# Mask and decay scores as one product of 88 rows a half, key-value products of 32 output rows

## What is computed

```python
log_f = log_sigmoid(fg); cs = cumsum(log_f)           # per head, over the tokens
log_D = where(tril, cs_s - cs_t, -inf) + ig_t         # mask and decay scores
D_mat = exp(log_D - max(log_D))
C = (q k^T / sqrt(32)) * D_mat
h = C / (max(|sum C|, exp(-max)) + 1e-6) @ v          # 8 heads of 32
x = x + tanh(g) * layernorm(h) * ln_scale
```

## Time and profile before

| | |
|---|---|
| three runs | 786.97, 788.75, 788.55 us; median 788.55 |
| profiled execution | 790.31 us, its span 788.5 us |
| PE busy | 678.9 us, 86% (weight loads 545.5, 69%) |
| DVE busy | 527.2 us, 67% |
| POOL busy | 404.8 us, 51% |
| ACT busy | 386.1 us, 49% |
| constants and gates | 0 to 57 us |
| hand-over | 57 to 85 us |
| attention loop, slots 0 to 31 | 85 to 295 us |
| routing | 295 to 350 us |
| experts | 350 to 788 us |

### The profile page before, as it was taken

One profiled execution on the slowest core, in us unless ns is written; L12 is line 12 of the kernel. 1 busy time (PEld: TensorE's weight loads), 2 busy tenths in 40 slices (PEclk: granted clock), 3 DMA queues, 4 the chain that ended last, 5 costly groups with the idle time before them and its releaser, 6 DMA issues.

```text
span 788.5 us, 17816 instructions
## 1 busy us (share of the span) xinstructions
PE 678.9 (86%) x6018; PEld 545.5 (69%) x6018; DVE 527.2 (67%) x1389; ACT 386.1 (49%) x973; POOL 404.8 (51%) x402
## 2 busy tenths in 40 slices
PE   1983889998899874068999999999999999999993
PEld 1541556665566663047998989988989899889893
DVE  8716899899998877964555565555555555655551
ACT  3533677777777763154344444343444443434441
POOL 5024499897989991021244453453444535444423
PEclk9995655557655655569999999999999999999997
DMA  9813789986998861173597897897988977969752
GB/s 283 270 37 122 198 267 263 297 280 208 298 300 254 269 209 54 29 307 108 166 289 238 265 281 253 232 315 213 281 259 245 291 253 234 315 200 305 231 147 49
DMA packets 85817, 179.70 MB, mean 228 GB/s; under 512 B 14881, under 2 KB 48546, under 8 KB 85730
## 3 DMA queue, kind: packets, MB, share of 16 engines
q1 hardware_dynamic: 63202, 140.10, 56.2%
q0 software_dynamic: 13824, 18.43, 10.8%
q10 hardware_dynamic: 8704, 20.06, 6.5%
HBM read 140.93 MB, written 38.67 MB: 228 GB/s over the span
## 4 chain that ended last, share of the span: by engine, by line
PE 57%; POOL 20%; issue 9%; DVE 9%; ACT 2%; DMA 2%; SPq 1%; POOLq 0%; DVEq 0%; ACTq 0%
PE bank L1096 49%; POOL whl L483 8%; POOL x L717 3%; POOL x L720 3%; POOL vp L561 3%; POOL qE L577 2%; PE bank L304 2%; PE bank L1090 2%; PE bank L307 2%; POOL kw L569 2%; DVE R L991 1%; PE bank L317 1%; DMA EB<-e_d 1%; DVE Qe L988 1%; PE bank L734 1%
## 5 line engine op out<-in xcount | busy, mean ns | idle before, releaser
L1096 PE MATMUL bank<-xh,w 128*128 128x256 bf16 (+1 forms) x1760 | 268.2, 263 | 9.7 <-DVE xl L1152 5.7
L1078 POOL DMA_INDIRECT out<-res,TS x72 | 115.4, 1603 | 214.9 <-DVE res L1213 130.9
L1096 PE MATMUL bank<-xl,w 128*128 128x256 bf16 (+1 forms) x880 | 222.5, 263 | 0.0
L1169 ACT ACTIVATE sg<-bank 128x256 f32<-128x256 f32 (+1 forms) x240 | 86.8, 362 | 230.3 <-PE bank L1096 226.6
L1096 PEld LDWEIGHTS bank<-xh,w 128*128 128x128 bf16 x1760 | 165.5, 98 | 28.5 <-issue 11.9
L1199 DVE TENSOR_TENSOR hf<-sg,bank 128x256 f32<-128x256 f32 (+1 forms) x200 | 78.9, 394 | 122.5 <-ACT sg L1169 117.4
L1096 PE MATMUL bank<-w,hh 128*128 128x256 bf16 x864 | 140.0, 273 | 0.0
L483 POOL TENSOR_TENSOR whl<-wst,whl 128x408 bf16<-128x408 f32 x96 | 94.0, 1006 | 61.2 <-ACT whl L468 61.1
L1069 POOL DMA_INDIRECT xg<-y_d,TG x72 | 72.7, 1010 | 79.0 <-DVE TS L1026 48.4
L1096 PE MATMUL bank<-w,hlo 128*128 128x256 bf16 x360 | 98.1, 273 | 0.0
L1163 ACT CAST hh<-hf 128x256 bf16<-128x256 f32 (+1 forms) x240 | 90.4, 377 | 12.9 <-DVE hf L1201 11.6
(11 more groups left out here) (222 smaller groups left out, 1107.4 us busy)
## 6 DMA issues: line engine op xcount, KB each, us to landing
w<-w_d SPq DMA_DIRECT2D x40, 1408.0 KB
w<-w_d SPq DMA_DIRECT2D x40, 768.0 KB
wst<-in_wts SPq DMA_DIRECT2D x32, 612.0 KB, 4.7
w_d<-whl ACTq DMA_DIRECT2D x32, 612.0 KB, 6.7
vb<-in_kv SPq DMA_DIRECT2D x8, 528.0 KB, 5.4
xa<-in_x SPq DMA_DIRECT2D x8, 512.0 KB, 8.5
kT<-in_kv SPq DMA_DIRECT2D x8, 512.0 KB, 8.9
xc<-in_x SPq DMA_DIRECT2D x8, 512.0 KB, 7.7
```

The lines of the kernel that those rows point to most:

```text
L1078: nc.gpsimd.indirect_dma_start(out, bass.IndirectOffsetOnAxis(ap=TS[:, c0:c0 + 1], axis=0), res[w][:, j, :], None, bounds_check=TOK - 1, o ...
L1096: mm = nc.tensor.matmul(dst, l, r, start=(n == 0), stop=(n == len(pairs) - 1))
L1169: nc.scalar.activation(sg[m % 2][0:K, 0:N], bank[0:K, 2 + (NM * w + m) % 4, 0:N], ACT.Silu).then_inc(f_sg, 1)
```

## The change

Three things change.

1. The mask goes into the decay product. `asb` and `mx` grow from 24 to 96 rows, of which 88 are used: rows 64 to 87 hold what rows 0 to 23 held, and rows 0 to 63 a mask for half a block: in `asb` an identity of 64 for the one half of the columns and zeros for the other, in `mx` the mask of 64 x 64. Row 0 is free in the mask (its entry never masks), so it carries the half of the block that is masked whole. There is one `asb` for each half u of the query tokens, and a product for each half: 88 rows, 4 heads x 64 columns, written in runs of 64. `b_am_sync` loads the decay rows of `asb` twice. POOL fills the new rows before the loop, with memsets and copies.
2. The state product is made head by head, 32 output rows and 33 columns each, straight into the diagonal blocks; the rest of the area is zeroed once by a memset on DVE. Ut and blkm go; the scale of 1/sqrt(32) moves into `col` (ACT's copy L348). St is updated from PSUM.
3. The constants for blkm go (one iota on POOL, three operations on DVE), and the waits are renumbered.

```diff
-        asb = [attn(f"asb{w}", [24, 2, S], BF16) ...]; mx = [attn(f"mx{w}", [24, 2, HG, S], BF16) ...]
+        asb = [attn(f"asb{w}", [96, 2, 2, S], BF16) ...]; mx = [attn(f"mx{w}", [96, 2, HG, S], BF16) ...]
 def consts_pool(pool):
-            nc.gpsimd.iota(blk[:, :]...)
...
             for w in range(2):
                 nc.gpsimd.memset(mx[w][:, :, :, :], 0.0).then_inc(s_mz, 1)
-                nc.gpsimd.memset(asb[w][:, :, :], 1.0).then_inc(s_mz, 1)
+                nc.gpsimd.memset(asb[w][:, :, :, :], 1.0).then_inc(s_mz, 1)
+            pool.wait_ge(s_mz, 4)
+            for w in range(2):
+                nc.gpsimd.memset(asb[w][0:64, :, :, :], 0.0).then_inc(s_tri, 1)
+            pool.wait_ge(s_const, NCONST)
+            pool.wait_ge(s_tri, 2)
+            for w in range(2):
+                for u in range(2):
+                    half = asb[w][0:64, u, :, :].rearrange("p g (c v s) -> p (g c) v s", c=NC, v=2)[:, :, u, :]
+                    nc.gpsimd.tensor_copy(half, identb[0:64, 0:64].unsqueeze(1).to_broadcast([64, 2 * NC, 64])).then_inc(s_tri, 1)
+                nc.gpsimd.tensor_copy(mx[w][0:64, :, :, :].rearrange("p g j (c s) -> p (g j c) s", s=64),
+                                      maskb[0:64, 0:64].unsqueeze(1).to_broadcast([64, 4 * NC * HG, 64])).then_inc(s_tri, 1)
+            pool.wait_ge(s_tri, 8)
+            for w in range(2):
+                nc.gpsimd.memset(asb[w][0:1, :, :, :], 0.0).then_inc(s_tri, 1)
+                nc.gpsimd.memset(mx[w][0:1, :, :, :], NEG).then_inc(s_tri, 1)
+            pool.wait_ge(s_tri, 12)
+            for w in range(2):
+                first = asb[w][0:1, 0, :, :].rearrange("p g (c v s) -> p (g c) v s", c=NC, v=2)[:, :, 1, :]
+                nc.gpsimd.memset(first, 1.0).then_inc(s_tri, 1)
-        NCONST = 16
+        NCONST = 13
 def consts_dve(dve):
-            nc.vector.tensor_scalar(blkt...); nc.vector.tensor_scalar(blkm...); nc.vector.tensor_tensor(blkm...)
 def g_actf_all(act):
-                    nc.scalar.copy(dst, src).then_inc(g_cols, 1)
+                    nc.scalar.activation(dst, src, ACT.Copy, scale=SCALE).then_inc(g_cols, 1)
 def g_pe_all(pe):
+            pe.wait_ge(b_uz, 1)
             b_s_pe(pe, 0)
             pe.wait_ge(s_sel, 2)
+            pe.wait_ge(s_tri, 14)
 def g_dvef(dve):
             V.memset(g2[:, 0:P], 0.0).then_inc(g_dve, 1)
+            V.memset(bank[:, 4:6, UO:UO + HG * DV], 0.0).then_inc(b_uz, 1)
 def b_am_sync(sp, b):
-            sp.dma_start(asb[w][0:12, :, :], a_d[...]...).then_inc(b_am[w], 16)
+            for u in range(2):
+                sp.dma_start(asb[w][64:76, u, :, :], a_d[...]...).then_inc(b_am[w], 16)
 def b_s_pe(pe, t):
-                    mm = nc.tensor.matmul(bank[:, 4 + g, UO:UO + HG * DV], kw[u % 2][:, g * P:(g + 1) * P],
-                                          vv(u)[:, g * HG * DV:(g + 1) * HG * DV], start=True, stop=True)
+                    for j in range(HG):
+                        hd = g * HG + j
+                        mm = nc.tensor.matmul(bank[DH * j:DH * (j + 1), 4 + g, UO + DV * j:UO + DV * (j + 1)],
+                                              kw[u % 2][:, DH * hd:DH * (hd + 1)], vv(u)[:, DV * hd:DV * (hd + 1)],
+                                              start=True, stop=True)
 def b_dl_pe(pe, t):
-                nc.tensor.matmul(dl, identb[:, :], maskb[...], start=True, stop=False)
-                nc.tensor.matmul(dl, asb[w][:, g, c * P:(c + 1) * P], mx[w][:, g, :, c * P:(c + 1) * P],
-                                 start=False, stop=True).then_inc(b_dl, 1)
+                dl = bank[:, g, :].rearrange("p (j v s) -> p j v s", j=HG, v=2)
+                for u in range(2):
+                    s0 = c * P + 64 * u
+                    mm = nc.tensor.matmul(dl[:, :, u, :], asb[w][0:88, u, g, c * P:(c + 1) * P], mx[w][0:88, g, :, s0:s0 + 64],
+                                          start=True, stop=True)
+                mm.then_inc(b_dl, 1)
 def b_st_dve(dve, t):
-                mask = blkm[:, :].unsqueeze(1).to_broadcast([P, 2, HG * DV])
+                ge(dve, b_h, t)
                 if c == 0:
-                    ge(dve, b_h, t)
-                    V.scalar_tensor_tensor(St[0][:, :, :], ub, SCALE, mask, ALU.mult, ALU.mult).then_inc(b_st, 1)
+                    V.tensor_copy(St[0][:, :, :], ub).then_inc(b_st, 1)
                 else:
-                    V.scalar_tensor_tensor(Ut[:, :, :], ub, SCALE, mask, ALU.mult, ALU.mult).then_inc(b_ut, 1)
...
                     for g in range(2):
                         ins = V.scalar_tensor_tensor(St[c % 2][:, g, :], St[1 - c % 2][:, g, :], dec[:, b, g, c:c + 1],
-                                                     Ut[:, g, :], ALU.mult, ALU.add)
+                                                     ub[:, g, :], ALU.mult, ALU.add)
```

More of the change, by code:

```diff
@@ L110, in build @@
         vb = [attn(f"vb{w}", [P, NC, NH * DV]) for w in range(2)]; qE = [attn(f"qE{w}", [P, D]) for w in range(2)]
-        asb = [attn(f"asb{w}", [24, 2, S], BF16) for w in range(2)]; mx = [attn(f"mx{w}", [24, 2, HG, S], BF16) for w in range(2)]
+        asb = [attn(f"asb{w}", [96, 2, 2, S], BF16) for w in range(2)]; mx = [attn(f"mx{w}", [96, 2, HG, S], BF16) for w in range(2)]
         vp = [attn(f"vp{w}", [P, 2, NH, DV], BF16) for w in range(2)]
         kw = [attn(f"kw{w}", [P, D]) for w in range(2)]; St = [attn(f"St{w}", [P, 2, HG * DV]) for w in range(2)]
-        Ut = attn("Ut", [P, 2, HG * DV])
         n1 = attn("n1", [P, NH]); n2 = attn("n2", [P, NH]); n3 = attn("n3", [P, NH])
@@ L217, in consts_dve @@
             nc.vector.memset(onesb[:, :], 1.0).then_inc(s_const, 1)
[L218 removed]
+            dve.wait_ge(s_iota, 4)
             nc.vector.tensor_copy(rowjb[:, :], rowj[:, :]).then_inc(s_const, 1)
@@ L223, in consts_dve @@
             nc.vector.tensor_scalar(maskb[:, :], rowj[:, :], pcol[:, 0:1], NEG, ALU.is_lt, ALU.mult).then_inc(s_const, 1)
[L224 to L227, removed]
+            dve.wait_ge(s_const, 9)
             nc.vector.tensor_tensor(selt[:, :], identf[0:12, 0:4], identf[0:12, 4:8], ALU.add).then_inc(s_const, 1)
-            dve.wait_ge(s_const, 13)
+            dve.wait_ge(s_const, 10)
             nc.vector.tensor_tensor(sel12[:, :], selt[:, :], identf[0:12, 8:12], ALU.add).then_inc(s_const, 1)
@@ L246, in mx_act @@
             act.wait_ge(s_mz, 2 * w + 1)
-            nc.scalar.copy(mx[w][0:12, :, :, :], sel12[:, :].unsqueeze(1).unsqueeze(3).to_broadcast([12, 2, HG, S])).then_inc(s_sel, 1)
+            nc.scalar.copy(mx[w][64:76, :, :, :], sel12[:, :].unsqueeze(1).unsqueeze(3).to_broadcast([12, 2, HG, S])).then_inc(s_sel, 1)
         def lsg_dve(dve):
@@ L505, in b_dl_pe @@
             w = b % 2
-            ge(pe, b_am[w], (b // 2 + 1) * 16 * (1 + HG))
+            ge(pe, b_am[w], (b // 2 + 1) * 16 * (2 + HG))
             for g in range(2):
                 ge(pe, b_D, 2 * t + g - 1)
-                dl = bank[:, g, :]
-                nc.tensor.matmul(dl, identb[:, :], maskb[:, :].unsqueeze(1).to_broadcast([P, HG, P]),
-                                 start=True, stop=False)
-                nc.tensor.matmul(dl, asb[w][:, g, c * P:(c + 1) * P], mx[w][:, g, :, c * P:(c + 1) * P],
-                                 start=False, stop=True).then_inc(b_dl, 1)
+                dl = bank[:, g, :].rearrange("p (j v s) -> p j v s", j=HG, v=2)
[4 more added lines that the diff above has]
+                mm.then_inc(b_dl, 1)
         def b_pv_pe(pe, t):
```

16 lines of the change are left out of this document (6 added, 10 removed).

## The result

The changed kernel takes 796.34 us (median of four runs, 795.88 to 798.23) beside 788.45 us for the kernel before on the same chip (786.97 to 788.75): ratio 1.0104, 95% interval 1.0083 to 1.0125. It is 1% slower. Forecast was 784.9 with a range up to 791.5, so the result lies outside it. The medians are 7.9 us apart. The profiled execution took 795.88 (span 794.1), 5.6 us more than the profiled one of before, and it is these 5.6 us that the traces explain.

The account below looks back on a forecast made before the run. POOL and PE at half clock were taken to pace the loop in turn. Loop -9.2, hand-over -0.5 and start +6 gave -3.7 us: 786.6 against the profiled 790.31, 784.9 against the median 788.55; range 778 to 791.5.

Parts of the forecast that it names:

- the one on the constants: Start of the kernel: constants end unchanged, then POOL's new fill holds DVE's q-normalisations; 6 us more, ends 0 and 9.
- So the constants end about where they did.: Very start: blkm's work leaves DVE, the asb memset doubles to 1.9 us, and held DVE operations finish as before.
- Two get through at each of its ends: Start: two held DVE operations pass whenever a POOL instruction ends; applied to normalisations 1 to 4, 6 us more.
- the rival in which the hold costs nothing: Start: normalisations not held by POOL, or PE's backlog covers them; 779.5 us, chance 0.20.
- The rival on the slower side: Turns 1 to 4, 20 to 45 us: normalisations held longer, PE's clock falls (+3.5); 791.4 us, chance 0.17.
- The loop: Attention loop, slots t = 0 to 31: 9.2 us less, ends 5 and 12, with items near 26.3 us.
- The St pair at 0.6 with POOL working: State update on DVE: two St operations reading PSUM take 0.6 us instead of 1.22 beside POOL.
- That DVE is part of the slot in which POOL waits for ACT's cast: Slot t = 17's kind: Cm comes 1.0 us earlier, the 1.0 us for which POOL waits.
- The scores at 1.1 us less PE a slot: Loop on PE: four products of 256 columns take 1.1 us instead of 2.20 for mask and decay scores.
- The key-value products at 1.0, no change: Loop on PE: 16 smaller records take 1.0 us, as now; low end 0.3, high end 4.2.
- Rival (c), dear new forms: Loop on PE: key-value or score products stay dear; 788.5 us, or 788.55 + 5.5 up to 802; chance 0.13.
- The hand-over: Between gates and loop: memset and extra load +0.7 us, scores before the loop -1.2; together 0.5 less.

Follow-up runs that it names:

- e1: Changed kernel with its first four POOL memsets on 32 rows instead of 96 and POOL waiting for `wwin` ahead of them; fill stays on POOL: 792.62 us.
- e7: Changed kernel with 32-row memsets, fill on DVE, and POOL's four memsets waiting until DVE's constants are done: 774.86 us.
- e2: Changed kernel with the fill of rows 0 to 63 moved from POOL to DVE, behind the last normalisation; 96-row memsets stay: 780.90 us.
- e11: Changed kernel with 32-row memsets and fill on DVE, but Ut back: DVE copies the short products to SBUF and St reads the copy: 786.68 us.
- e5: Changed kernel with 32-row memsets and fill on DVE, but the old mask and decay scores, two products for each g: 779.35 us.
- e9: Kernel before with only the head-by-head key-value products (no Ut, no blkm); its own scores, 24 rows, no fill: 779.82 us.

## Why the prediction was wrong

**The step that failed is the one on the constants**, in both of its halves.

*"So the constants end about where they did."* They ended at 16.8 instead of 11.6, 5.2 us later. I had rightly added the longer `asb` memsets, but I took from the earlier trace rows that a held operation gets through at every end of a POOL instruction. In the changed kernel `rowjb` missed four ends in a row. The rows showed only ends that were taken; nothing in them excluded one that is missed, and I priced the term at nothing without a bound on that side. Why these ends were missed stays open; e1 and e7 show only that without the chain of memsets `rowjb` takes 0.67.

*"Two get through at each of its ends"*, 6 us for the normalisations with ends 0 and 9. The form was right, L290 is held for microseconds; the count was not. Two had got through in the earlier trace rows, where the operations have 128 columns; of the four with 256 columns in normalisation 0 one got through at each end, so it took four ends, 9.89 us, where my rule gives two. I also had it pass before the fill bit, as in the trace of before (17.20 to 18.58): the late constants and the held L255 pushed it to 23.91, into the fill. There PE has no earlier turn to work on, and the delay goes nearly whole into the first gate product, 17.1 us late. e1 and e2 take the two apart: 3.7 us of time for the gap and the rows, 15.4 for the fill, and with both the time is 779.29, close to the 779.5 of the rival in which the hold costs nothing. The copies on POOL took 3.59 for 4096 elements, my low end, not 4.9; with that alone the hold would have been shorter than predicted.

The rival on the slower side named this place and 791.4, and its first half, normalisations that are held longer, is what happened, but not by longer copies. Its sign, turns at the slower rate after 30 us, is there as well: four transposes in 1.12 us at 33.85, eight in 1.95 at 38.14, where eight later take 1.04. But these are turns 0 and 1, which took as long before (1.97 and 1.94, at 18 and 21 us), only later. The granted clock reads 1.00 in both kernels from there to the end of the gates. So the slower rate adds little, 3.58 us for the first gate product against 3.27, and not the 3.5 of that rival.

**The loop** was right in size, and DVE's part in it was right. Predicted were 9.2 us less and items of 26.3; measured 10.3 and 26.13. Term by term:

- The St pair at 0.6 with POOL working: 0.60. That DVE is part of the slot in which POOL waits for ACT's cast: shown by e11. POOL's waits for that cast fell from 13.8 us to 2.2, and are 13.5 in e11.
- The scores at 1.1 us less PE a slot: 2.20 became 0.83, so 1.4 less. The drain rule that I quoted from the Trainium skill (TensorEngine Tiling (Array Packing), Key Properties) gave 1.3 and is the better of the two estimates here; no run shows the drain itself. But the term is worth nothing in the kernel that has the state update (e5, e9), which the prediction had half said ("an engine that, below, no longer sets most slots").
- The key-value products at 1.0, no change: 0.38. The nearest row that I used only as the low end (0.3) was the right one. This is why the new scores became superfluous: an item has these products in three of its four slots, so the 27.86 us of an item that PE paced lose 3 x 0.66 here already and come to 25.9, an estimate, under the 26.1 of POOL's.
- PE no longer paces the loop, as forecast: it is busy 125.01 of 156.81 us. Rival (c), dear new forms, is refuted. The output in runs of 64 columns costs nothing: 0.21 us for 256 columns at half clock is 1.2 columns a nanosecond. The Trainium skill (PSUM — Partial Sum Buffer, Specifications) says that a non-contiguous pattern slows matmuls; for this pattern the trace doesn't agree.

**The hand-over** gained 1.9 where 0.5 was forecast. The PSUM memset took 0.28 as priced (0.3), and the first score product still waits 4.67 us for the loads of `mx` against 4.20; the gain lies behind it: from that product to slot t = 0 it was 9.6 us before and is 7.2, 2.4 less, where I had counted 1.2 for the scores in that stretch. What the 1.2 beyond it consists of I can't say; the shorter key-value products stand in the same stretch.

So against 790.31: start +17.4 (predicted +6), hand-over -1.9 (-0.5), loop -10.3 (-9.2), behind the loop +0.4: +5.6 where -3.7 was the sum.

## What to carry to other kernels

Filling buffers "before the loop, where POOL is idle" is not free when DVE works there: POOL's memsets and copies held DVE's fp32 casts and tensor_scalars, and what stood behind them, from one instruction of POOL (3.6 us) up to a whole chain of them (11.06 us). Put POOL's setup behind DVE's constants, or give the fill to DVE itself if it has an idle stretch. And when two engines pace a loop in turn, ask for each part of a change whether the other part alone already brings its engine under the second pacemaker: here one part (e9) was worth the whole gain of the loop, and the other, not needed beside it (e5, e9), brought the fill, the larger part of the cost.

## What was not expected of the hardware

- One DVE cast of 128 columns stood for 11.06 us through four POOL memsets in a row, past four ends of a POOL instruction; in other kernels it missed none, one or two. Which ends let a held operation through isn't settled: the rows, the gap in POOL's queue and the moment at which DVE's operation comes all differ between these kernels.
- How many held operations one end lets through differs too: two of 128 columns (`identb` and `upperb`, ending at 6.02 and 6.09), one of 256 (the four of L290).
- POOL's time for a memset or copy of 4096 bf16 elements doesn't depend on the rows: 3.64 us for 1 row, 3.53 for 32, 3.59 for a copy of 64, 3.50 for 96. DVE copies the same 64 x 4096 in 1.20 us.
- Products of 32 output rows and 33 columns follow each other closely: 16 records in 0.38 us at half clock, 24 ns each, beside 260 ns for the records of 128 rows and 132 columns in the earlier trace rows. That is less than the 27.5 ns which 33 columns at 1.2 GHz would take one after the other (an estimate by one column a cycle, the rate of the scores), so they seem to overlap.
